# Lane sums by matmul, one pass of row maxima per half, maxima items from step 0, and q's decay on VectorE, in a two-layer attention kernel

## What is computed

```python
# layer 0, attention: B, T, C = 2, 1024, 128; H = 16, D = 8
att = einsum('bhtd,bhsd->bhts', q, k) / sqrt(D) + alibi_causal_mask
y = einsum('bhts,bhsd->bhtd', softmax(att), v) ; x = x + y @ W_proj + b_proj  (residual)
# layer 0, feed-forward
beta = mean(abs(weight)); w_q = clip(round(weight / (beta + EPS)), -1, 1)
gamma = max(abs(xn))                       # over all tokens and channels
xq = clip(xn * 128 / gamma, -128 + EPS, 128 - EPS)
y = (xq @ w_q) * (gamma * beta / 128)
# layer 1, attention: 16 chunks of 128 tokens (8 per batch), 16 heads of 64
scores = (qi @ ki^T) * mask
o = scores @ vi + (qi * q_dec) @ kv        # q_dec: q's decay
kv = blk_dec * kv + (ki * k_dec)^T @ vi
```

## Time and profile before

| | |
|---|---|
| median of three runs | 600.23 us |
| the profiled execution | 600.33 us, of which the span from first to last instruction is 598.6 us |
| PE busy | 479.1 us, 80% of the span |
| DVE busy | 359.2 us, 60% |
| ACT busy | 240.0 us, 40% |
| POOL busy | 236.5 us, 40% |
| mean granted TensorE clock | 0.911 |
| layer 0 (to the last `pv`) / layer 1 | 324 us / 275 us |

### The profile page before, as it was taken

How to read it: one execution, slowest core, us unless ns; L and a number is a source line. 1 busy time by engine, 2 the same in 40 slices (tenths; PEclk the granted TensorE clock), 3 DMA queues, 4 the chain that set the end, 5 groups by cost and what they waited for, 6 DMA issues and landing times.

```text
span 598.6 us, 8401 instructions
## 1 busy us (share of the span) xinstructions
PE 479.1 (80%) x2998; PEld 192.6 (32%) x2998; DVE 359.2 (60%) x638; ACT 240.0 (40%) x460; POOL 236.5 (40%) x315
## 2 busy tenths in 40 slices
PE   7786787878774878776878974997499899999896
PEld 3352122222221221221424521453134443444442
DVE  5777587888883874857343859545526617641430
ACT  2574368777763865766563111111001111111110
POOL 2033225342212636312102565167407932993520
PEclk9998599999997995989995987878689999999999
DMA  6630512242020201000000311100001301210000
GB/s 202 224 92 16 175 38 97 60 182 60 3 60 2 61 2 42 20 2 2 2 0 1 123 72 53 53 29 25 2 18 71 106 0 72 88 37 0 18 2 18
DMA packets 19085, 31.78 MB, mean 53 GB/s; under 512 B 2544, under 2 KB 7120, under 8 KB 18724
## 3 DMA queue, kind: packets, MB, share of 16 engines
q1 hardware_dynamic: 19044, 31.24, 16.2%
HBM read 13.20 MB, written 8.06 MB: 36 GB/s over the span
## 4 chain that ended last, share of the span: by engine, by line
PE 49%; DVE 8%; issue 5%; ACT 5%; DMA 2%; SPq 1%; POOL 1%; ACTq 0%; DVEq 0%; POOLq 0%
PE PS L658 6%; PE PS L812 6%; PE PS L799 5%; PE PS L845 5%; PE PS L818 5%; PE PS L773 4%; PE PS L640 4%; ACT prob L1340 4%; PE PS L831 2%; DVE sm L1195 2%; PE PS L581 1%; DMA turned<-by_sin 1%; DVE xn L960 1%; PE PS L585 1%; PE PS L781 1%
## 5 line engine op out<-in xcount | busy, mean ns | idle before, releaser
L1340 ACT ACTIVATE prob<-PS 128x512 f32<-128x512 f32 (+1 forms) x320 | 160.0, 552 | 78.2 <-PE PS L640 74.9
L1043 DVE TENSOR_REDUCE pmax<-PS 128x8 f32<-128x1024 f32 x128 | 153.4, 1222 | 57.4 <-PE PS L581 31.6
L640 PE MATMUL PS<-q_op,k_op 55*128 55x512 bf16 (+3 forms) x384 | 63.0, 348 | 50.9 <-ACT prob L1340 42.7
L1492 POOL TENSOR_SCALAR_AFFINE_SELECT prob<-prob 128x512 f32<-128x512 f32 x64 | 39.9, 637 | 142.2 <-ACT prob L1340 142.1
L658 PE MATMUL PS<-prob,vaug 128*16 128x512 f32 (+3 forms) x768 | 86.9, 542 | 0.0
L1538 POOL TENSOR_TENSOR vdec<-vk,c_sb 128x256 f32<-128x256 f32 x56 | 32.6, 616 | 96.9 <-ACT vk L1364 96.9
L1407 ACT COPY oT<-PS 128x512 f32<-128x512 f32 x32 | 18.8, 586 | 124.5 <-PE PS L818 108.2
L581 PE MATMUL PS<-k_op,q_op 52*128 52x128 bf16 (+3 forms) x576 | 60.2, 288 | 7.2 <-DVE pmax L1043 5.3
L640 PEld LDWEIGHTS PS<-q_op,k_op 55*128 55x128 bf16 x384 | 18.4, 94 | 138.2 <-ACT prob L1340 112.4
L1195 DVE TENSOR_TENSOR sm<-PS,c_sb 128x512 f32<-128x512 f32 x64 | 41.2, 685 | 33.6 <-PE PS L799 33.4
L799 PE MATMUL PS<-qr,kr 64*128 64x512 f32 x128 | 39.7, 699 | 20.5 <-DVE sm L1195 16.4
(11 more groups left out here) (172 smaller groups left out, 568.4 us busy)
## 6 DMA issues: line engine op xcount, KB each, us to landing
turned<-by_sin SPq DMA_DIRECT2D x80, 128.0 KB, 2.0
k_op<-k_scr SPq DMA_DIRECT2D x14, 220.0 KB
q_op<-q_scr SPq DMA_DIRECT2D x14, 208.0 KB
c_sb<-const_dram SPq DMA_DIRECT2D x1, 2576.0 KB, 8.4
q_scr<-part_a SPq DMA_DIRECT2D x6, 256.0 KB, 3.4
k_scr<-part_a SPq DMA_DIRECT2D x6, 256.0 KB, 3.8
q_scr<-part_b SPq DMA_DIRECT2D x6, 256.0 KB, 3.1
k_scr<-part_b SPq DMA_DIRECT2D x6, 256.0 KB, 3.4
```

The lines of the kernel that those rows point to most:

```text
L640: last = mm(PS[:, (GH * s + h) % ST_BANKS, at:at + nn], k_op[rows, slot, h // 2, P * j:P * j + P], q_op[rows, slot, h // 2, P * i0:P * i0 ...
L1043: vec.tensor_reduce(dst, both.rearrange("p a (b c) -> p a b c", c=P), AX.X, ALU.max, negate=(r not in PLACE)).then_inc(done, 1)
L1340: sca.activation(prob[:, s % P_SLOTS, h, 0:UNIT_W[u]], PS[:, k % ST_BANKS, 0:UNIT_W[u]], ACT.Exp).then_inc(s_exp, 1)
```

## The change

- The two reductions over the lanes become matmuls: item `lanes` (a transpose of the lane maxima into one row, and the sum by a matrix of ones) in step 36, of which DVE copies the sum and takes the maximum of the row, and item `spread` (that maximum to all lanes) in step 37. `scales` moves to step 38, `ternary` to step 39.
- `pmax` has one range per row tile, padded with -3e38, so that `maxima` is one pass per half (4 x 4 rows of 6, or of 8). `dneg` goes. `ORDER` sets the order of the row tiles, which the `turn` item undoes.
- The items ahead of the loop are step -1; step 0 has five items of its own. The steps after that get two items each from step 3 on. `turn` (n, 0) stands after max item 10 of group n, `turn` (n, 1) after max item 3 of group n + 1, so that they fall on steps 10n - 5 and 10n + 1. The last maxima items stand in step 68, `turn` (7, 1) in step 69, ahead of the yt items.
- `quantise` moves from POOL to DVE, one piece for each batch, in steps 72 and 73. `fade_q` moves from POOL to DVE, behind the fourth `masked` of a chunk, in the last chunk of a span to its end.

```diff
-MAXIMA = [{0: (6, 7, 1), 1: (0, 6, 5), 2: (7, 10, 1), 3: (1, 5, 1)},
-          {4: (24, 28, 1), 5: (19, 24, 1), 6: (28, 33, 1), 7: (12, 19, 1)}]
+ROW = [6, 8]
+PLACE = {0: (3, 6), 1: (11, 1), 2: (22, 1), 3: (27, 9), 4: (32, 1), 5: (37, 1), 6: (41, 1), 7: (48, 1), 8: (28, 1)}
-SOON, FULL_STEP = 32, 70
+SOON, LATER_RATE = 27, 2
-            if u == 2 and n:
+            if n and u == 3:
                 out.append(("turn", n - 1, 1))
-            if u == NR0 * PAIRS + 1:
+            if u == NR0 * PAIRS + (4 if n else 1):
                 out.append(("turn", n, 0))
+            if n == NG and u in (13, 15):
+                out.append((("lanes", "spread")[u == 15], 0, 0))
-        n_paced = min(n, FIRST_ITEMS + ITEM_RATE * s, SOON + max(0, s - 2) * (n - SOON) // (FULL_STEP - 2))
+        n_paced = min(n, FIRST_ITEMS + ITEM_RATE * (s + 1), SOON + LATER_RATE * s)
...
+                    elif kind == "lanes":
+                        pe.wait_ge(s_gmax, 1)
+                        pe.wait_ge(s_pads, 2)
+                        mm(o[0:1, 0, 0:P], small[:, 1:2], W["ident"], start=True, stop=True)
+                        last = mm(o[:, 1, 0:1], ones[:, :], small[:, 0:1], start=True, stop=True)
+                    elif kind == "spread":
+                        used(pe, ITEM_AT["lanes", 0])
+                        last = mm(o[:, 0, 0:1], ones[0:1, :], small[0:1, 11:12], start=True, stop=True)
...
+            def quantise(b):
+                link(vec.tensor_scalar(xn2T[:, cs], xn2T[:, cs], small[:, 5:6], top_q, ALU.mult, ALU.min))
+                vec.tensor_scalar(xn2T[:, cs], xn2T[:, cs], -top_q, None, ALU.max).then_inc(s_clip, 1)
...
-                if half == 0:
-                    note(vec.tensor_reduce(pmax[:, :, 32], pmax[:, :, 10:12], AX.X, ALU.max))
-                for i, (a, b_, step) in MAXIMA[half].items():
-                    last = vec.tensor_reduce(rmax[:, :, i], pmax[:, :, a:b_:step], AX.X, ALU.max, negate=True)
-                    last = vec.tensor_tensor(rmax[:, :, TPS:], rmax[:, :, TPS:], dneg[:, :, :], ALU.min)
+                rows = pmax[:, :, ROWS_AT[half]:ROWS_AT[half] + ROW[half] * TPS]
+                vec.tensor_reduce(rmax[:, :, TPS * half:TPS * half + TPS], rows.rearrange("p h (i w) -> p h i w", w=ROW[half]),
+                                  AX.X, ALU.max, negate=True).then_inc(s_rmax, 1)
...
                 masked(c, 2)
                 masked(c, 3)
+                if ch < TPS - 1 and c + 1 < NCH:
+                    fade_q(c + 1)
                 rope(i + 1, f[1:3])
                 advance(c)
                 rope(i + 1, f[3:])
+                if ch == TPS - 1 and c + 1 < NCH:
+                    fade_q(c + 1)
...
-            def whole_sums():
-                po.partition_all_reduce(small[:, 2:3], small[:, 0:1], P, RED.add).then_inc(s_gall, 1)
-                po.partition_all_reduce(small[:, 3:4], small[:, 1:2], P, RED.max).then_inc(s_gall, 1)
```

More of the change, by code:

```diff
@@ L166 @@
 FFN_STEP = LARGEST_STEP[-1] + 1
-TERNARY_STEP = FFN_STEP + 3
-Q_STEPS = [s for s in range(TERNARY_STEP + 2, NSTEP) if all(j != i0 for j, i0, _ in UNITS[s % NU][1])][:8]
-QW = B * T // len(Q_STEPS)
+SCALES_STEP = step_of(ITEM_AT["spread", 0]) + 1
+QUANTISE_STEP = [72, 73]
 LN1_STEP = step_of(ITEM_AT["back", 1]) + 1
@@ L1041, in item @@
                     of_pair = slice(2 * pair, 2 * pair + 2)
-                    dst = pmax[:, of_pair, PLACE[r]:PLACE[r] + TPS] if r in PLACE else dneg[:, of_pair, :]
-                    vec.tensor_reduce(dst, both.rearrange("p a (b c) -> p a b c", c=P), AX.X, ALU.max,
-                                      negate=(r not in PLACE)).then_inc(done, 1)
+                    at, step = PLACE[r]
+                    if k == ITEM_AT["max", 0]:
+                        v.wait_ge(s_pads, 1)
+                    vec.tensor_reduce(pmax[:, of_pair, at:at + step * (TPS - 1) + 1:step],
+                                      both.rearrange("p a (b c) -> p a b c", c=P), AX.X, ALU.max).then_inc(done, 1)
                     if (n, 0) in LAST_MAX and k in (LAST_MAX[n, 0], LAST_MAX[n, 1]):
@@ L1058, in item @@
                     add_to_x(n, both[:, 0, :]).then_inc(done, 1)
+                elif kind == "lanes":
+                    note(vec.tensor_copy(small[:, 2:3], both[:, 1, 0:1]))
+                    vec.tensor_reduce(small[0:1, 11:12], both[0:1, 0, 0:P], AX.X, ALU.max).then_inc(done, 1)
+                elif kind == "spread":
+                    vec.tensor_copy(small[:, 3:4], both[:, 0, 0:1]).then_inc(done, 1)
                 elif kind == "xn1T":
@@ L1299, in _ @@
             root(B, rstd2)
-            sca.activation(small[:, 11:12], W["bk"], ACT.Exp)
+            sca.activation(small[:, 12:13], W["bk"], ACT.Exp)
             for k, (name, i) in enumerate(UB):
@@ L1434, in third @@
                 po.tensor_tensor(part_of(m, 2), rest[:, m - NSPAN, :], part_of(m, 1), ALU.subtract).then_inc(s_part[2], 1)
-            def quantise(k):
-                cs = slice(QW * k, QW * k + QW)
-                top_q = 128.0 - 1e-5
-                g_.wait_ge(s_ffn, 1)
-                po.tensor_scalar(xn2T[:, cs], xn2T[:, cs], small[:, 5:6], top_q, ALU.mult, ALU.min).then_inc(s_scaled, 1)
-                g_.wait_ge(s_scaled, k + 1)
-                po.tensor_scalar(xn2T[:, cs], xn2T[:, cs], -top_q, None, ALU.max).then_inc(s_clip, 1)
             n_split = [0]
```

91 lines of the change are left out of this document (41 added, 50 removed).

## The result

The changed kernel takes 572.9 us (median of 4 runs, 569.55 to 575.83) beside 600.06 us for the kernel before (4 runs, 599.78 to 604.24). The ratio is 0.953, with a 95% interval of 0.946 to 0.960. The forecast was 573.8 us, in a range of 564 to 588. The profiled execution took 574.82 us.

The account below looks back on a forecast made before the run. Layer 0 was bound by PE and ACT waiting for each other, plus stalls and slow clock; layer 1 mostly by PE's own work. Terms sum to -26.5 us against the profiled 600.33: 573.8 us, range 564 to 588.

Parts of the forecast that it names:

- The reload: Step 41: POOL's 7.32 us idle after the lane reductions goes, so the step falls from 10.77 to 2.75 us, -8.0.
- The turns and the clock behind them: Earlier half-1 turns remove the step 51 stall with its slow clock, -7.8, and second the step 62 stall, -3.2.
- The last turn: Steps 69 and 70: PE waits about 1.9 us for POOL's parts, both steps take 8.1 us, -3.5 taken.
- 3.45 us for a step with a yt item: Length assumed for step 70 in the changed kernel, added to step 69's 2.75 + 1.9 us.
- a rival with 1 in 6: Slow clock comes back elsewhere, behind step 69's wait or the busy start: 6.0 to 7.8 us, at most 581.6; chance 0.17.
- The opening: First steps of layer 0: step 3 starts 1.0 us earlier, steps 3 and 4 shorten by 3.8, +1.5 back: -3.3.
- as the slow stretch then lasts for one step more: Start of layer 0: steps 3 and 4 take 8.5 us at slow clock, with one further slow step, +1.5.
- Lanes and spread: Steps 36 and 37 hold three items, with small matmuls and DVE passes added: +1.2, bounds 0 to 2.5.
- ahead of the DMAs on SP stand only loads that have long been free: SP's queue at the half-1 turns: nothing ahead delays mrow's DMAs, leaving 0.2 us waits in four groups, +0.8.
- Maxima: Layer 0: single pass saves 16 times some 0.4 us of DVE, mostly under the loop: -1.0.
- Quantise: Steps 72 and 73: four passes on DVE cost at most 5.5 us in all; 0 to +3, +0.5 taken.
- The decay: Layer 1, 14 chunks: q's decay on DVE instead of POOL, gains in chunks 1 and 3: -2.2, bounds -4 to +14.

Follow-up runs that it names:

- the last comparison: Changed kernel with operand loads issued first, lanes in step 69, last turn and spread in step 70, against the changed kernel run again: 564.7 us beside 574.04 us.

## Why the prediction came out right, point by point

- **The reload** (-8.0): step 41 lost 7.5 us. Alone it gave -7.1 with its items, undone +5.0 with more slack around it. The idle came back with the reductions, at the first `tensor_tensor` behind them: 6.96 us. The traces agree with what the prediction took from the Trainium skill, GPSIMD Engine Reference, section 2.1, a cost with no visible instruction, with 7.32 and 6.96 us for the page's some 6. With the page's figure the term is -6.7 and not -6.8. The split now comes in step 39, not in step 41.
- **The turns and the clock behind them** (-7.8, -3.2): the wait of 0.19 us and the clock at 1.00 in steps 51 to 57 are as forecast. Steps 58 to 68 gave 1.4 us of the second term: steps 62 and 63 gave 3.0, about as summed, and step 67 another 0.5. But step 64 took 4.27 us, 1.2 more than before, at half clock, and step 59 lost 0.9 to its loads. When the same kernel ran again for the last comparison, step 64 took 2.78 us, so this stretch is not the kernel's own.
- **The last turn** (-3.5): the mechanism and the wait were right (1.67 for 1.9), the step "3.45 us for a step with a yt item" failed. Step 70 took 5.00 us at half clock. I had named that as a rival with 1 in 6 and priced it at 6.0 to 7.8 us; it cost 2.6, and when the same kernel ran again 1.3 (8.90 us for both steps). With the same wait at full clock the two steps took 7.55 us, where I had 8.1.
- **The opening** (-3.3): mis-sized, -5.7. The start of step 3, which I put 1.0 us earlier, came 0.8 later (64.64 for 63.88). What failed is the step "as the slow stretch then lasts for one step more": steps 3 and 4 took 3.11 and 2.77 us, not 8.5 in all and 1.5 behind them. The slow stretch had run out before step 3. That is the bound with no further slow step, which the range had (by the prediction's own numbers it lies 4.5 us lower, 3.0 in the two steps and 1.5 behind them, where it says 3.3). But this is not always so: when the same kernel ran again, the clock was at 0.50 once more from 64.79 on for 6.83 us, steps 3 and 4 took 3.77 and 4.19 us and step 5 began at 71.90, for a gain of 4.3. Of the ten traces with this opening five have that second stretch (step 5 at 71.48 to 71.90) and five not (70.52 to 71.09). So the gain is 4.3 to 5.7 us. The stretch in the changed kernel:

```profile
49.73:59.97 10.24, 8.33 (x52) 2.38 (x54) 7.65 (x8) 3.43 (x8) 3.43 (x8) 0.50 0.01 2
```

- **Lanes and spread** (+1.2): steps 36, 37 and 41 had 2.4 us more than a free step, of which step 36 had 0.54 before the change as well (3.29 us); moved away they gave 1.4 net. It lies in the bounds of 0 to 2.5, at the upper half. In step 41 PE waits 0.69 us for DVE's max pass ahead of the turn, which stands behind five passes of `ternary`.
- **The operand loads**: the failed step is the sentence that ahead of the DMAs on SP stand only loads that have long been free. I looked at what stands ahead of `mrow` and not at what is queued behind it: the next group's operands, which cost 2.4 us in four steps. The term was missing altogether, and was paid for by the opening.
- **Maxima** (-1.0): -0.7 to -1.5 by one trace, and not told from nothing. **Quantise** (+0.5): 0.
- **The decay** (-2.2): -2.6 and -2.8. The size is right, and the reason for half of it. The `w_sb` pass beside POOL's `qd` gave its 2.0 us. Of chunk 1, which was to give 1.1, little can be said, since its time jumps by 1.3 us between kernels with the same layer 1; chunks 1 to 3 together gave 0.6. A `qd` pass on DVE takes 1.22 us alone, below the bound of twice the 0.69 us. The wait beside a POOL addition, up to 1.3 us more in the forecast, came in two of the 14 passes (2.35 us, +1.1) and cost nothing: chunks 6 and 10, in which they lie, take no longer than before. Beside the rule from the Trainium skill, SBUF — State Buffer, section "Who interferes with whom", the prediction sets 8.07 against 2.14 us, which are passes with one tensor input (`x_sb`; `mv` and `rstd` are one value per partition). The case with two inputs, for which the page states it, is the `w_sb` pass, 2.71 against 0.69.

By stretches the errors are -2.4 (opening), +0.6, -0.3, +1.6 (step 64 and the loads), +2.6 (last turn) and -1.1 (from step 71 on): +1.0 in all. The total is nearer than its parts deserve.

## What to carry to other kernels

A transfer that is moved behind a later semaphore takes everything with it that is queued behind it on the same queue: for every moved step, list what stands behind it as well as what stands ahead. A wait of PE of 1.7 us was worth 1.6 us here where the clock stayed up behind it and 4.3 where it fell; put an item where its input is surely there, even a step later, if nobody wants it sooner. And judge a change of a few microseconds by the steps that it touches: whole-kernel times of the changed kernel spread by 6 to 7 us, those of the kernel before by 10 to 13.
